# Sending the first layer's expert rows a chunk at a time instead of a batch at a time

## The chip, the cores and the metric

One NeuronCore of a Trainium2 chip runs the whole kernel. The metric is device time in microseconds (us), the median of several executions. Besides them one execution was taken by the hardware profiler.

## The reference, cut to what matters

Sixteen batches of 112 tokens, 256 wide, go through four residual blocks: cross attention with 16 heads over 375 keys, a top-2 mixture of 8 experts with a capacity of 560 rows an expert, a masked attention with one head, and a second top-2 mixture. The change lies at the seam of the first two:

```
x = x + xattn0(layernorm(x), ctx)            # 16 heads, 375 keys
# then, for t = layernorm(x) seen as T = 1792 tokens:
logits = t @ wr.T;  vals, idx = top_k(logits, 2);  gating = softmax(vals)
pos    = cumsum(mask) - 1;  keep = mask & (pos < 560)
xg     = rows of t gathered expert by expert (8 x 560)
x      = x + segment_sum(gate * (gelu(xg @ w1 + b1) @ w2 + b2))
```

## The kernel before, in words

The engines run separate programs that meet at semaphores. `attention0` is written as one long list of steps, `batch_order()`, which yields pairs (b, h) for b from 0 to 19 and h from 0 to 15. At step (b, h) TensorE (PE) makes the scores of head h of batch b, and, some steps behind, the probabilities (L505 to L508) and the values (L521) of an earlier head. The other engines walk the same list, each doing what its program names for a step. A pair (b, h) is thus a place in the order of an engine's queue and not a time: GpSimd (POOL), which has little to do, stands far ahead of PE and waits at its semaphores.

In the list of POOL stand, for each b: at h = 4 and 5 of odd b the norm of two coming batches (`pool_rsqrt`, `pool_normed`, L1715 to L1722), at h = 9 `context_lo(b + 2)` (L1749), which waits for ScalarE (ACT), at h = 10 the norm after attention of batch b - 2, which waits for VectorE (DVE), and `pool_scatter` for some (b, h).

Routing goes by chunks of batches, `CHUNKS0 = ((0, 4), (4, 4), (8, 4), (12, 2), (14, 1), (15, 1))`, as (first, count). When the logits of a chunk are there, DVE works out for its tokens the rows of the expert buffer that they go to (`dest`, L1167, semaphore `r_dest`) and the gates, which it writes beside the token in `XN` (L1194, semaphore `r_gate`). `pool_scatter(e, 0, b)` waits for both of the chunk of b and then issues two indirect DMAs (L1739), one for each of a token's two experts. Each writes 112 rows of 268 f32 words from `XN[:, b]` to `xg_scratch` in DRAM, 120 KB, so 240 KB a batch. Eight semaphores `d_sc` take turns: the DMAs of batch b wait until those of batch b - 4 have landed. All descriptors of POOL go through queue q0; the loads and stores that SP issues go through q1, on the same 16 DMA engines.

SP's part of attention 0 is a chain for each batch: `write_k` and `write_q` (L1941) store the split keys and queries to DRAM, `stack_k` (L1955) and `stack_q` (L1973) read them back in another layout into `KST` and `QST`, and `minima_rows` (L1982) writes two small rows into `QST` for each eight heads. PE waits for these at L483 and L505. After the last batch SP's `gathered(0)` (L2090) waits for all the scatters of the layer, and PE turns what it loads (L588).

`pvo_done` counts the turned values of a batch on DVE (L1363): its 17th is the one of batch 15.

Of the kernel before, what the change touches and what calls it, by code (L numbers as in the profile page):

```python
# [13 lines left out]
B, S, D, KEYS = 16, 112, 256, 375  # L14
# [45 lines left out]
CHUNKS0 = ((0, 4), (4, 4), (8, 4), (12, 2), (14, 1), (15, 1))  # L60
# [18 lines left out]
def build_kernel(nc, x, ctx_n, ctx_t, mask, bmask, wq, wk, wv, wo, wrt, w1, b1, w2, b2, gw, v1, v2, v3, const, out):  # L79
    top = ExitStack()  # L80
    with top:
# [3 lines left out]
        def sem(name):  # L85
            return top.enter_context(nc.semaphore(name))
# [91 lines left out]
        def expert_buffers(n):  # L178
# [41 lines left out]
        qk_done, min_done, pr_done, exp_done, pv_done, pvo_done, orm_done, xadd_done = (sem(n) for n in (  # L220
            "qk_done", "min_done", "pr_done", "exp_done", "pv_done", "pvo_done", "orm_done", "xadd_done"))
# [122 lines left out]
        def batch_order():  # L344

            return [divmod(n, H) for n in range(N + 4 * H)]
# [15 lines left out]
        def ends_chunk(b):  # L362
            return next((i for i, (b0, nb) in enumerate(CHUNKS0) if b0 + nb - 1 == b), None)
# [1347 lines left out]
        def pool_rsqrt(e, i, n, var_sem, rs_sem):  # L1711
            e.wait_ge(var_sem, n)
            if n > 2:
                e.wait_ge(rs_sem, n - 2)
            e.tensor_scalar(rs[:, i:i + 1], st2[:, i, 1:2], EPS, None, ALU.add).then_inc(eps, 1)  # L1715
            Chain.eps += 1
            e.wait_ge(eps, Chain.eps)
            e.tensor_tensor(rs[:, i:i + 1], rs[:, i:i + 1], epsm[:, 1:2], ALU.pow).then_inc(rs_sem, 1)

        def pool_normed(e, i, b, rs_sem, xn_sem):  # L1720
            e.wait_ge(rs_sem, b + 1)
            e.tensor_scalar(XN[:, b, 0:D], X[:, b, :], st2[:, i, 0:1], rs[:, i:i + 1], ALU.subtract, ALU.mult).then_inc(xn_sem, 1)  # L1722

        def pool_scatter(e, layer, b):

            dst, bound = ((xg_d, ROWS), (xg2_d, ROWS2))[layer]
            c = next(i for i, (b0, nb) in enumerate((CHUNKS0, CHUNKS1)[layer]) if b0 <= b < b0 + nb)
            e.wait_ge(r_dest, layer * len(CHUNKS0) + c + 1)
            e.wait_ge(r_gate, layer * len(CHUNKS0) + c + 1)
            if b == 0:  # L1730
                if layer == 0:
                    e.wait_ge(d_z, 16 * (E + 1))
                else:
                    e.wait_ge(d_z2, 16 * 2 * E)
            for d in range(2):
                n = 2 * (B * layer + b) + d
                if n >= 8:
                    e.wait_ge(d_sc[n % 8], 16 * (n // 8))
                e.indirect_dma_start(  # L1739
                    out=dst.ap()[0:bound, :], out_offset=bass.IndirectOffsetOnAxis(ap=dest[:, d, b:b + 1], axis=0),  # L1740
                    in_=XN[:, b, 0:RW], in_offset=None, bounds_check=bound - 1, oob_is_err=False).then_inc(d_sc[n % 8], 16)

        def pool_attention0(e):
            e.memset(CT[:, :, :, KEYS:KP], 0.0).then_inc(setup, 1)
            e.memset(epsm[:, 1:2], -0.5).then_inc(setup, 1)

            def context_lo(b):
                e.wait_ge(ch_done, b + 1)
                e.tensor_tensor(CL[:], CT[:, b % 2, :, :], CH[:], ALU.subtract).then_inc(cl_done, 1)  # L1749

            e.memset(VV[:, :, :, :, HD:HD + 1], 1.0).then_inc(setup, 1)
            e.memset(zero[:], 0.0).then_inc(setup, 1)
            e.wait_ge(setup, 4)
            e.memset(zero[:, :, RW_ID:RW_ID + 1], 1.0).then_inc(setup, 1)
            for i in range(2):
                e.wait_ge(setup, 5 + i)
                e.memset(KST[ROWS_KQ:ROWS_KQM, i].bitcast(F32), -1.0).then_inc(setup, 1)
            e.wait_ge(setup, 7)
            for b in range(2):
                pool_rsqrt(e, b, b + 1, var1, rs1)  # L1760
            e.memset(MK[:, 1, :].bitcast(F32), 0.0).then_inc(setup, 1)
            e.memset(XN[:, :, RW_ID:RW], 0.0).then_inc(setup, 1)
            e.iota(toki[:], [[S, B]], base=0, channel_multiplier=1).then_inc(setup, 1)
            e.wait_ge(setup, 10)
            e.tensor_copy(XN[:, :, RW_ID].bitcast(I32), toki[:]).then_inc(setup, 1)
            e.wait_ge(setup, 11)
            e.memset(QST[:, 1].bitcast(F32), 0.0).then_inc(stack_z, 1)
            e.wait_ge(stack_z, 2)
            e.memset(KST[ROWS_KQ:ROWS_KQM, 2].bitcast(F32), -1.0).then_inc(setup, 1)
            e.wait_ge(setup, 12)  # L1770
            for b in (2, 3):
                pool_rsqrt(e, b % 2, b + 1, var1, rs1)
            scattered_at = {(b + 7, 6): b for b in range(8)}
            scattered_at.update({(B - 1, 6): 8, (B - 1, 13): 9, (B, 6): 10, (B, 13): 11,
                                 (B + 1, 6): 12, (B + 1, 7): 13, (B + 2, 6): 14, (B + 3, 6): 15})
            for b, h in batch_order():
                if b + 2 < B and h == 9:
                    context_lo(b + 2)
                if b % 2 and b + 3 < B and h in (4, 5):
                    pool_rsqrt(e, h - 4, b + h, var1, rs1)  # L1780
                    pool_normed(e, h - 4, b + h - 1, rs1, xn1)
                if 2 <= b <= B + 1 and h == 10:
                    pool_rsqrt(e, 2 + (b - 2) % 2, b - 1, var2, rs2)
                    if b < B + 1:
                        pool_normed(e, 2 + (b - 2) % 2, b - 2, rs2, xn2)
                sent = scattered_at.get((b, h))
                if sent is not None:
                    if sent == B - 3:
                        e.wait_ge(pvo_done, B + 1)
                    pool_scatter(e, 0, sent)  # L1790

        def pool_experts(e, layer, between=None, beside=iter(())):
            base, per = (0, 4) if layer == 0 else (4 * E, 6)
# [399 lines left out]
        @block.gpsimd  # L2193
        def _(e):
            def first_block():
                pool_overflow_add(e, 0, range(5 * E - 5 - NY, 5 * E - 5))

            pool_attention0(e)
            pool_experts(e, 0, lambda: pool_roots(e, 1))
            pool_attention1(e, 2)  # L2200
            pool_experts(e, 1, first_block, pool_overflow_loads(e, 0))
            overflow_blocks(e, lambda j: pool_overflow(e, j))
# [53 lines left out]
```

## Time and profile before

| | |
|---|---|
| runs shown | 1006.34, 1006.79, 1010.84 us, median 1006.79 us |
| profiled execution | 1006.79 us, span 1004.7 us, so 2.1 us lie around the span |
| TensorE busy | 911.1 us, 91% of the span, 7913 matmuls |
| VectorE, ScalarE, GpSimd busy | 681.5, 439.0 and 473.9 us |
| mean granted TensorE clock | 0.959 |
| queue q0 / q1 of the DMAs | 18.33 / 140.40 MB, 9.1% / 52.6% of the 16 engines' span |

Attention 0 takes about the first 360 us, the first experts the next 230, attention 1 and its routing up to about 676, the second experts the rest.

How to read it: times are counted from the span's start. A busy share of PE is that of modelled, pipelined matmuls. A row of the timeline gives start, duration, engine, line, operation, output and input; in brackets stands how long the engine was idle ahead of it and what ended the idle time. A DMA that POOL issues shows up as the time that POOL takes over its descriptors, and not as that of the transfer.

### The profile page before, as it was taken

The page shows a single profiled execution, that of the slowest core. Times are in us where ns is not written, and L with a number is a line of the kernel's source. Part 1 is how long each engine was busy: PE and PEld are TensorE (multiplying, and loading weights), DVE is VectorE, ACT ScalarE, POOL GpSimd, SP SyncE. Part 2 cuts the span into 40 slices and gives each one's busy share as a digit, 9 for nine tenths or more (in the row PEclk, how much of TensorE's full clock was granted, in tenths as well). Part 3 has the DMA queues.
Part 4 walks back from the last instruction along what each step waited for, and adds up shares of the span by engine and source line. Part 5 has one row for each costly group of instructions (what it writes and reads, how often), then busy time and mean ns, then how long its engine had stood idle before and what let it go on. Part 6 is the DMA issues. An engine that isn't in the chain of part 4 may idle for free. (4 is left out here: it accounts for less than half of the span.)

```text
span 1004.7 us, 22213 instructions
## 1 busy us (share of the span) xinstructions
PE 911.1 (91%) x7913; PEld 839.8 (84%) x7913; DVE 681.5 (68%) x1988; ACT 439.0 (44%) x924; POOL 473.9 (47%) x443
## 2 busy tenths in 40 slices
PE   5799999999999749999999979838999999999996
PEld 5688988888888538999999957628999999999886
DVE  5667677667768448777777558846787777777353
ACT  3255555555554335555564434314333343442220
POOL 6024125244322426667666433672635655544513
PEclk8799999999999959999999999968999999999999
DMA  7998888797894167878977666634535465433202
GB/s 197 185 224 179 215 222 220 200 223 187 214 226 120 45 189 193 196 185 203 225 179 188 150 165 187 210 113 129 151 86 147 105 229 133 121 96 99 22 4 25
DMA packets 111840, 160.42 MB, mean 160 GB/s; under 512 B 12640, under 2 KB 100032, under 8 KB 109792
## 3 DMA queue, kind: packets, MB, share of 16 engines
q1 hardware_dynamic: 97776, 140.40, 52.6%
q0 software_dynamic: 13936, 18.33, 9.1%
q8 instruction: 78, 1.28, 0.5%
q14 instruction: 50, 0.41, 0.2%
HBM read 103.45 MB, written 56.96 MB: 160 GB/s over the span
## 5 line engine op out<-in xcount | busy, mean ns | idle before, releaser
L377 PE MATMUL ps<-XGH,WH 128*128 128x280 f32 (+1 forms) x768 | 220.2, 287 | 3.8 <-DVE GT L1488 2.4
L377 PE MATMUL ps<-XGL,WH 128*128 128x280 f32 (+1 forms) x768 | 221.1, 288 | 0.0
L377 PE MATMUL ps<-XGH,WL 128*128 128x280 f32 (+1 forms) x768 | 220.6, 287 | 0.0
L1804 POOL TENSOR_TENSOR HTL<-GT,HTH 128x280 fp32r<-128x280 f32 x112 | 114.5, 1024 | 164.8 <-DVE HTH L1492 164.8
L1341 DVE CUSTOM_DVE_ANT_0 NS<-ps,negm 112x375 f32<-112x375 f32 x256 | 135.2, 540 | 52.0 <-PE ps L483 48.6
L377 PE MATMUL ps<-WH,HTH 128*128 128x256 f32 (+1 forms) x536 | 152.8, 285 | 2.5 <-POOL HTL L1804 2.4
L377 PEld LDWEIGHTS ps<-XGH,WH 128*128 128x128 f32 x768 | 147.5, 192 | 5.2 <-DVE GT L1488 3.6
L377 PE MATMUL ps<-WL,HTH 128*128 128x256 f32 (+1 forms) x536 | 150.4, 281 | 0.0
L377 PE MATMUL ps<-WH,HTL 128*128 128x256 f32 (+1 forms) x536 | 150.2, 280 | 0.0
L377 PEld LDWEIGHTS ps<-XGH,WL 128*128 128x128 f32 x768 | 147.5, 192 | 0.0
L377 PEld LDWEIGHTS ps<-XGL,WH 128*128 128x128 f32 x768 | 147.1, 192 | 0.0
L876 ACT ACTIVATE PT<-ps 125x448 f32<-125x448 f32 x192 | 104.3, 544 | 76.8 <-PE ps L508 66.4
L1492 DVE CAST HTH<-GT 128x280 fp32r<-128x280 f32 x256 | 111.7, 443 | 16.4 <-ACT GT L949 9.6
L952 ACT ACTIVATE GT<-ps 128x280 f32<-128x280 f32 x128 | 51.7, 404 | 127.3 <-PE ps L377 124.8
L377 PEld LDWEIGHTS ps<-WH,HTH 128*128 128x128 f32 (+1 forms) x536 | 99.2, 185 | 3.5 <-DVE XG L1505 3.0
L483 PE MATMUL ps<-KST,QST 96*112 96x376 f32 x256 | 95.5, 379 | 4.5 <-DMA QST<-q_scratch 3.0
L377 PEld LDWEIGHTS ps<-WL,HTH 128*128 128x128 f32 (+1 forms) x536 | 99.5, 186 | 0.0
L377 PEld LDWEIGHTS ps<-WH,HTL 128*128 128x128 f32 (+1 forms) x536 | 99.3, 185 | 0.0
L1071 DVE TENSOR_TENSOR WL<-WG,WH 128x1024 fp32r<-128x1024 f32 x60 | 79.3, 1324 | 15.8 <-ACT WH L810 11.1
L1749 POOL TENSOR_TENSOR CL<-CT,CH 128x752 fp32r<-128x752 f32 x14 | 25.1, 1795 | 130.9 <-ACT CH L823 130.8
L1816 POOL DMA_INDIRECT out<-XG x40 | 67.1, 1678 | 38.1 <-DVE XG L1507 31.1
L810 ACT ACTIVATE WH<-WG 128x1024 fp32r<-128x1024 f32 x80 | 83.1, 1051 | 3.0 <-PE ps L377 3.0
(227 smaller groups left out, 1983.4 us busy)
## 6 DMA issues: line engine op xcount, KB each, us to landing
WG<-in_v SPq DMA_DIRECT2D x48, 512.0 KB
KST<-k_scratch SPq DMA_DIRECT2D x48, 376.0 KB
WG<-in_w SPq DMA_DIRECT2D x32, 512.0 KB
k_scratch<-KHL SPq DMA_DIRECT2D x64, 188.0 KB
CT<-in_ctx_t SPq DMA_DIRECT2D x28, 375.0 KB, 4.5
xg_scratch<-zero SPq DMA_DIRECT2D x8, 1289.8 KB
xg_scratch<-zero SPq DMA_DIRECT2D x16, 586.2 KB, 7.9
XG<-xg_scratch SPq DMA_DIRECT2D x14, 536.0 KB, 3.8
```

The lines of the kernel that those rows point to most:

```text
L377: m = e.matmul(out_ap, l, r, start=n == 0, stop=n == len(steps) - 1)
L483: e.matmul(ps[0:S, n % 3, 0:KP], QST[0:ROWS_KQ, b // 2 % 2, j // 4, up, j % 4, o:o + S], KST[0:ROWS_KQ, b % NKST, j, :], start=True, stop= ...
L810: e.activation(WH[n % NR][:], WG[:, n % NSTG, :], ACT.Copy).then_inc(wh_done, 1)
L876: e.activation(PT[:, k % 2, c, :], ps[0:KC, 3 + n % 2, 0:GQ], ACT.Exp, scale=-1.0).then_inc(exp_done, 1)
L952: e.activation(GT[:, gi % NG, :], ps[:, 2 * gi % 4, 0:HALF], ACT.Silu).then_inc(g_act[1], 1)
L1071: e.tensor_tensor(WL[n % NR][:], WG[:, n % NSTG, :], WH[n % NR][:], ALU.subtract).then_inc(wl_dve, 1)
L1341: e.tensor_tensor_reduce(out=NS[:, n % 2, :], in0=ps[0:S, n % 3, 0:KEYS], in1=negm[:], scale=1.0, scalar=3.0e38, op0=ALU.add, op1=ALU.min, ...
L1492: e.tensor_copy(HTH[:, f, cols], g).then_inc(hh[layer], 1)
L1749: e.tensor_tensor(CL[:], CT[:, b % 2, :, :], CH[:], ALU.subtract).then_inc(cl_done, 1)
L1804: e.tensor_tensor(HTL[:, f, cols], GT[:, gi % NG, :], HTH[:, f, cols], ALU.subtract).then_inc(hl_pool[layer], 1)
L1816: e.indirect_dma_start(out=(x_d.ap()[:, :], out2)[layer], out_offset=bass.IndirectOffsetOnAxis(ap=XG[0:rows_of(c), ex % 2, c, RW_ID:RW_ID ...
```

## The change

The table `scattered_at`, which gave each batch of the first layer a step for its scatter, goes. In its place a chunk's batches are sent in the list of four batches after its last one, at h = 6, 11, 13 and 15, or at h = 6 and 7 for b = 17. A wait for `pvo_done` ahead of the scatter of batch 13 goes too. The work is the same, 32 indirect DMAs in the same order.

| batch | step before | step after |
|---|---|---|
| 0, 1, 2, 3 | (7,6) (8,6) (9,6) (10,6) | (7,6) (7,11) (7,13) (7,15) |
| 4, 5, 6, 7 | (11,6) (12,6) (13,6) (14,6) | (11,6) (11,11) (11,13) (11,15) |
| 8, 9, 10, 11 | (15,6) (15,13) (16,6) (16,13) | (15,6) (15,11) (15,13) (15,15) |
| 12, 13, 14, 15 | (17,6) (17,7) (18,6) (19,6) | the same, without the wait at 13 |

```diff
@@ -1770,9 +1770,6 @@
             e.wait_ge(setup, 12)
             for b in (2, 3):
                 pool_rsqrt(e, b % 2, b + 1, var1, rs1)
-            scattered_at = {(b + 7, 6): b for b in range(8)}
-            scattered_at.update({(B - 1, 6): 8, (B - 1, 13): 9, (B, 6): 10, (B, 13): 11,
-                                 (B + 1, 6): 12, (B + 1, 7): 13, (B + 2, 6): 14, (B + 3, 6): 15})
             for b, h in batch_order():
                 if b + 2 < B and h == 9:
                     context_lo(b + 2)
@@ -1783,11 +1780,12 @@
                     pool_rsqrt(e, 2 + (b - 2) % 2, b - 1, var2, rs2)
                     if b < B + 1:
                         pool_normed(e, 2 + (b - 2) % 2, b - 2, rs2, xn2)
-                sent = scattered_at.get((b, h))
-                if sent is not None:
-                    if sent == B - 3:
-                        e.wait_ge(pvo_done, B + 1)
-                    pool_scatter(e, 0, sent)
+                turns = (6, 7) if b == B + 1 else (6, 11, 13, 15)
+                if b >= 4 and h in turns and ends_chunk(b - 4) is not None:
+                    b0, nb = CHUNKS0[ends_chunk(b - 4)]
+                    i = turns.index(h)
+                    if i < nb:
+                        pool_scatter(e, 0, b0 + i)
```

## Rows read from the trace of the kernel before

**Rows 1.** Engine times of the page: busy us, share of the span, instructions.

```profile
PE 911.1 (91%) x7913; PEld 839.8 (84%) x7913; DVE 681.5 (68%) x1988; ACT 439.0 (44%) x924; POOL 473.9 (47%) x443
```

**Rows 2.** Stretches: length, busy us (instructions) of each engine, clock, DMA share, GB/s.

```profile
176.00:180.00 4.00, 3.54 (x30) 3.26 (x23) 1.70 (x7) 1.57 (x4) 1.98 (x2) 1.00 0.94 237
...
256.00:260.00 4.00, 3.56 (x27) 3.38 (x26) 2.59 (x5) 2.94 (x6) 0.95 (x1) 1.00 1.01 266
...
280.00:284.00 4.00, 4.00 (x51) 3.63 (x51) 3.04 (x12) 1.82 (x5) 0.00 (x0) 1.00 1.08 236
...
332.00:336.00 4.00, 2.82 (x39) 2.34 (x40) 2.25 (x12) 2.63 (x7) 0.00 (x0) 1.00 0.08 24
```

**Rows 3.** Waits from 160 to 370 us: total us, times, longest.

```profile
ACT PT L876 <- remote: 3.6, 1, 3.6
...
PEld ps L505 <- DMA QST<-ML: 1.8, 4, 0.8
```

**Rows 4.** The same waits of PE's weight loads, from 280 to 300 us alone.

```profile
PEld ps L505 <- DMA QST<-ML: 0.8, 1, 0.8
PEld ps L483 <- DMA KST<-k_scratch: 0.6, 1, 0.6
```

**Rows 5.** Timeline of POOL, from batch 1's scatter to batch 6's.

```profile
176.06 1.03 POOL L1739 DMA_INDIRECT xg_scratch<-XN,dest  x1 [0.18 <-issue]
177.40 0.95 POOL L1739 DMA_INDIRECT xg_scratch<-XN,dest  x1 [0.30 <-issue]
192.43 1.81 POOL L1749 TENSOR_TENSOR CL<-CT,CH 128x752 fp32r<-128x752 f32 x1 [14.08 <-ACT CH L823]
...
254.89 1.03 POOL L1739 DMA_INDIRECT xg_scratch<-XN,dest  x1 [0.18 <-issue]
...
271.26 1.80 POOL L1749 TENSOR_TENSOR CL<-CT,CH 128x752 fp32r<-128x752 f32 x1 [14.09 <-ACT CH L823]
...
275.46 1.03 POOL L1739 DMA_INDIRECT xg_scratch<-XN,dest  x1 [0.18 <-issue]
```

**Rows 6.** Timeline of POOL, scatters of batches 8 to 15 and what stands between.

```profile
315.95 1.04 POOL L1739 DMA_INDIRECT xg_scratch<-XN,dest  x1 [4.13 <-issue]
...
326.59 1.03 POOL L1739 DMA_INDIRECT xg_scratch<-XN,dest  x1 [0.18 <-issue]
...
329.18 0.94 POOL L1739 DMA_INDIRECT xg_scratch<-XN,dest  x1 [0.30 <-issue]
330.42 0.94 POOL L1739 DMA_INDIRECT xg_scratch<-XN,dest  x1 [0.30 <-issue]
339.35 0.24 POOL L1715 TENSOR_SCALAR rs<-st 112x1 f32<-112x1 f32 x1 [7.99 <-DVE st L1290]
...
341.76 1.04 POOL L1739 DMA_INDIRECT xg_scratch<-XN,dest  x1 [0.18 <-DVE dest L1167]
...
349.34 0.94 POOL L1739 DMA_INDIRECT xg_scratch<-XN,dest  x1 [2.80 <-DVE OT L1363]
...
353.17 0.24 POOL L1715 TENSOR_SCALAR rs<-st 112x1 f32<-112x1 f32 x1 [1.65 <-DVE st L1290]
...
360.65 0.94 POOL L1739 DMA_INDIRECT xg_scratch<-XN,dest  x1 [3.98 <-DVE dest L1167]
361.89 0.94 POOL L1739 DMA_INDIRECT xg_scratch<-XN,dest  x1 [0.30 <-issue]
```

**Rows 7.** Timeline of DVE: gates of chunks 2 and 3, rows of chunk 5.

```profile
314.90 0.19 DVE L1194 TENSOR_TENSOR XN<-r_x 112x32 f32<-112x32 f32 x1
...
342.36 0.18 DVE L1194 TENSOR_TENSOR XN<-r_x 112x16 f32<-112x16 f32 x1
...
359.69 0.17 DVE L1167 TENSOR_SCALAR dest<-tq 112x2 int32<-112x2 f32 x1
```

**Rows 8.** Timeline of SP's queue: DMAs as issued.

```profile
290.24 1.25 SPq L1955 DMA_DIRECT2D KST<-k_scratch  x3
...
364.61 1.40 SPq L2090 DMA_DIRECT2D XG<-xg_scratch  x3
```

## The prediction

> **What bounds the kernel now.** I read the engine times first: TensorE is busy for 91% of the span [rows 1], so a gain has to take away one of its waits, and a loss has to make one. Then I read the stretches in which scatters are issued now or will be. In attention 0 PE is busy for 3.5 to 4.0 of each 4 us, at the full clock, while the 16 DMA engines are busy for 0.94 to 1.08 of the time [rows 2]. (A share over 1 is two queues' packets counted together.) From about 320 us on this turns over: the DMA engines are nearly idle (0.08), and PE's work is broken by waits. So there are two places to look at. One is the middle of attention 0, where moved transfers could make SP's loads late. The other is the end, where the last scatter releases the gather of the experts. Third come the waits of 160 to 370 us: DMAs that PE waits for are small there, 1.8 us over four waits for the minima rows [rows 3], the longest of them, 0.8 us, between 280 and 300 us, where the one wait for keys stands too, 0.6 us [rows 4]. Last, the timelines of POOL, DVE and SP's queue tell which scatter is late for what.
>
> **The end first, since it sets when the experts start.** The last two scatters start at 360.65 and 361.89 [rows 6]. The first was released by the `dest` of chunk 5, which DVE finishes at 359.86 [rows 7]. The gather goes out at 364.61 [rows 8], 1.78 us after POOL is done with the last one (361.89 + 0.94). All of this hangs on DVE's chain for batch 15, and none of it on POOL's place in its list. POOL is idle for 3.98 us ahead of it. The change leaves step (19,6) as it is. Cost: 0, as long as POOL reaches that step before 359.86, and now it reaches it 3.98 us early.
>
> **The scatters one by one.** A pair takes 1.34 us from its first start to its second [rows 5], and in a row without a wait the starts are 1.25 us apart [rows 6]. Four in a row have that pitch from 327.93 to the end of the 330.42 one, so I count 2.5 us for a pair that is added to a row.
>
> - Chunk 0. Batch 1 starts at 176.06 right behind the norm of step (7,10), though its step was (8,6): POOL is far ahead. In the new list it has the same place. Batches 2 and 3 follow at 178.65 and 181.15, until 183.3. The next work of POOL, L1749, waits for ACT until 192.43 after 14.08 us of idle time [rows 5]. Of that idle time 5.0 us are now filled, and 9 us are left. Cost to POOL's successors: 0. Without that cover it would be 5.0 us on the way to the next key projection.
> - Chunk 1 has the same form: batch 5 stays at 254.89, batches 6 and 7 come at 257.5 and 260.0, until 262.1. The next L1749 waits until 271.26, 14.09 us idle, 9 left. Cost 0.
> - Chunk 2. Batch 8 waits for its gates, done at 315.09 [rows 7], and starts at 315.95, 0.86 us later. Batch 9 sits behind the norm of (15,10), which waits for DVE. It stays at 326.59, with batch 10 at 329.18, and batch 11 moves from 341.76 to 331.67, until 333.9. POOL's next operation waits for DVE until 339.35 with 7.99 us of idle time [rows 6]. Cost 0: 5.5 us are left.
> - Chunk 3. Its gates are done at 342.54 [rows 7]. With the 0.86 us of chunk 2, batch 12 starts at 343.40 and batch 13, with no wait for DVE's turned values, at 345.95 instead of 349.34, and POOL is free at 348.1. The next, the root at 353.17, waits for DVE. Gain: 0 on any path, since batch 14 is behind that root and batch 15 behind its `dest`. The 2.80 us that the removed wait costs POOL are only turned into idle time a little later.
>
> Five pairs move far (2, 3, 6, 7, 11), two a little (12, 13), nine not at all. The semaphores `d_sc` add no wait: inside a group of four batches eight DMAs use eight different ones, and the batch four places back went out over 15 us earlier each time (the closest are 9 at 326.59 and 13 at 345.95).
>
> **What the transfers themselves cost.** A pair is 2 x 112 x 268 x 4 bytes, 0.24 MB. Two pairs more, 0.48 MB, fall into 178 to 184, where the engines move about 237 GB/s, and again into 257 to 262, at 266 GB/s [rows 2]. If the engines have no room at all, everything that SP has under way then lands up to 0.48 / 0.237 = 2.0 and 0.48 / 0.266 = 1.8 us later. That is 3.8 us as the upper bound, if PE was waiting for just that in both. Nothing in the waits says that it is: the minima rows hold PE up by at most 0.8 us at a time, and the keys once, between 280 and 300 us [rows 3, 4]. I take 0.2 us.
>
> On the other side four pairs leave places that are as full. Batch 6's went out at 275.46 [rows 5], ahead of the stretch from 280 with a DMA share of 1.08 [rows 2]. In that stretch the keys of batch 14 are written, and only at 290.24 does SP get to load them again [rows 8]. PE's one wait for keys, 0.6 us, and its longest for minima rows, 0.8 us, stand around it [rows 4]. The lower bound is both gone, -1.4 us. I take -0.4 us, nearer to zero, because 0.24 MB is one microsecond of a backlog of several.
>
> Sum: 1006.79 (the profiled execution, which is also the median of the runs) + 0 (end) + 0 (POOL) + 0.2 - 0.4 = 1006.6 us.
>
> The Trainium skill, DMA: Bandwidth & Descriptors, "Queues, rings and completion order", says that each DMA engine takes turns between the queues that have work, a packet at a time. By that rule a burst on q0 gets its turn ahead of whatever lies queued on q1, minima rows too. It speaks against this change, and no row of before separates the two queues at such a moment. By the rule the sum would have the 3.8 us of the next part.
>
> **The rivals.**
>
> 1. The bursts make PE wait. Mechanism: 0.48 MB of q0 is served between SP's packets at 178 to 184 and 257 to 262, the stores of keys and queries and the rows behind them land later, and PE stands at L483 or L505. For it: shares of 0.94 and 1.01 already. Against it: `stack_k` is issued about ten us ahead of its batch, and the waits seen come at other times. Price 2.0 + 1.8 = 3.8 us, 1010.6 us. It decides once the loads have less than 2 us in hand. It passes the half per cent (5.0 us) only if keys and queries both come late in one burst.
> 2. ACT's one wait that the profile calls remote, 3.6 us [rows 3], lies from 328.8 to 332.4. It contains the descriptors of batch 10 (329.18 to 331.36), and PE runs dry behind it. Should POOL's issuing be what holds ACT there, then the third pair in a row lengthens it by its 2.5 us, 1009.3 us. Against it: it is the only wait so named, and the other 30 indirect DMAs of this layer lie beside ACT's work without one. Should it be a matter of chance, it can as well be gone, -2.7 us or 1004.1 us.
> 3. The removed wait pays: batch 13's descriptors and DVE's chain for batch 15 (turned values at 347.8, then scale and turn back) no longer lie on each other at 349.3. Price: if a DVE step of 0.4 us was doubled by it, -0.4 us, 1006.4 us. Or the reverse, a clash with PE's last values before 347.8, +0.5 us.
> 4. The change does less than it says, because the list gives only an order: true for nine of 16 pairs, and already in the sum.
>
> **How the numbers follow.** The forecast, nothing that can be measured, has 0.70; rival 1 has 0.13, rival 2 longer 0.05 and shorter 0.04, rival 3 within the forecast's width 0.08. A measurement of this kernel can tell a change from none at about 0.5%, 5.0 us. No single mechanism reaches that. I leave 0.07 for slower by more (rival 1 with both loads late) and 0.03 for faster. The range: below, 1006.6 less the rest of the 1.4 us that can be gained and a microsecond for the runs' own spread, 1004.6; above, the full 3.8 us of rival 1, 1010.6, which also takes in the highest of the runs shown.
>
> **What would show it.** In the changed kernel's timeline of POOL scatters stand in rows at 176 to 183, 255 to 262 and 327 to 334, 1.25 us apart, with 9, 9 and 5.5 us of idle time behind them; no scatter near 208, 215, 275, 293. Batch 12 starts at about 343.4, batch 13 at about 346. The last two stand at 360.65 and 361.89, and the gather at 364.6, give or take a microsecond. The waits of L505 and L483 for DMAs stay under 3 us together. It is wrong if L1749 or the roots start behind a scatter instead of behind ACT or DVE, if PE's waits for `KST` or `QST` grow by microseconds right after 184 or 262, or if the gather of the experts starts over a microsecond later while DVE's chain does not.

## The result, and the profile after

| | before | after |
|---|---|---|
| median of 6 runs each, same chip | 1009.29 us (1006.34 to 1017.53) | 1020.58 us (1013.70 to 1025.14) |
| ratio, with 95% interval | | 1.011 (1.0077 to 1.0145) |
| profiled execution / its span | 1006.79 / 1004.7 us | 1021.98 / 1020.0 us |

The changed kernel is slower by 1.1%, about 11 us. The forecast was 1006.6 us and no change.

The engine times of the page do not show it. PE was as busy as before [rows 1], over a longer span:

```profile
PE 917.8 (90%) x7913; PEld 845.7 (83%) x7913; DVE 680.0 (67%) x1988; ACT 440.5 (43%) x924; POOL 474.9 (47%) x443
```

The timeline of POOL, to be held against [rows 5] and [rows 6], tells where the time is. The columns are start, duration, engine, line, operation.

```profile
175.26 1.03 POOL L1739 DMA_INDIRECT xg_scratch<-XN,dest  x1 [0.18 <-issue]
...
181.60 0.94 POOL L1739 DMA_INDIRECT xg_scratch<-XN,dest  x1 [0.30 <-issue]
...
196.71 1.82 POOL L1749 TENSOR_TENSOR CL<-CT,CH 128x752 fp32r<-128x752 f32 x1 [14.16 <-ACT CH L823]
...
264.94 0.94 POOL L1739 DMA_INDIRECT xg_scratch<-XN,dest  x1 [0.30 <-issue]
...
276.27 1.81 POOL L1749 TENSOR_TENSOR CL<-CT,CH 128x752 fp32r<-128x752 f32 x1 [10.39 <-ACT CH L823]
...
330.44 1.03 POOL L1739 DMA_INDIRECT xg_scratch<-XN,dest  x1 [0.17 <-issue]
...
336.79 0.95 POOL L1739 DMA_INDIRECT xg_scratch<-XN,dest  x1 [0.30 <-issue]
...
349.58 0.24 POOL L1715 TENSOR_SCALAR rs<-st 112x1 f32<-112x1 f32 x1 [11.85 <-DVE st L1290]
...
353.65 1.03 POOL L1739 DMA_INDIRECT xg_scratch<-XN,dest  x1 [1.84 <-issue]
...
357.49 0.94 POOL L1739 DMA_INDIRECT xg_scratch<-XN,dest  x1 [0.30 <-issue]
...
372.36 0.94 POOL L1739 DMA_INDIRECT xg_scratch<-XN,dest  x1 [3.97 <-DVE dest L1167]
```

POOL does what was foretold: unbroken rows with starts 1.25 us apart (2.15 us once, at 261.54), and idle time behind each. But what it waits for comes later. L1749 of step (8,9) started at 192.43 and is now at 196.71, that of (12,9) was at 271.26 and is at 276.27, the root of (16,10) was at 339.35 and is at 349.58. POOL is not late: it is idle for 14, 10 and 12 us ahead of these. ACT and DVE are late.

Behind the row at 176 the kernel is 5.0 us later than ahead of it (the step ahead, L1749 of (7,9), came 0.7 us early), behind the row at 257 it is 2.3 us, behind the one at 330 6.4 us, and by the gather another 1.5. Between the rows 2.7 us come back. The gather of the experts starts at 376.36 instead of 364.61 [rows 8], 11.75 us late.

The waits of 160 to 370 us, to be held against [rows 3] (total, times, longest), name the loss:

```profile
ACT PT L876 <- remote: 8.5, 3, 6.5
...
DVE NS L1341 <- issue: 5.8, 4, 4.5
...
DVE OT L1363 <- remote: 4.2, 1, 4.2
...
ACT KHL L839 <- remote: 1.7, 2, 0.9
...
PEld ps L505 <- DMA QST<-ML: 1.3, 2, 1.0
```

The wait for the minima rows is smaller than before, 1.3 us for 1.8, and none for keys is left. So SP's transfers are not what came late. What has grown are waits put down to "remote" or "issue", which is no engine of this core and no DMA that the profile shows (before had 3.6 us of them for ACT's PT and 3.0 us for DVE's NS). The long ones stand beside the rows. ACT is held from 332.6 to 339.15, while POOL issues from 330.44 to 337.74. DVE is held from 355.35 to 359.55, with POOL issuing from 353.65 to 358.43. In each the engine goes on 1.1 to 1.4 us after the last issue has ended. The 3.6 us of [rows 3] fit in: they end at 332.40, 1.0 us after the row of four that ends at 331.36.

TensorE shows best what is missing. A group at L521 is 24 matmuls of one head group, with no wait inside. Timeline of PE in the changed kernel:

```profile
181.27 0.56 PE L521 MATMUL ps<-PT,VV 125*17 125x112 f32 x10
182.63 0.39 PE L521 MATMUL ps<-PT,VV 125*17 125x112 f32 x4 [0.81 <-issue]
184.07 0.54 PE L521 MATMUL ps<-PT,VV 125*17 125x112 f32 x10 [1.05 <-issue]
```

The same group in the kernel before, where no scatter is under issue:

```profile
182.64 0.77 PE L521 MATMUL ps<-PT,VV 125*17 125x112 f32 x24
```

24 matmuls took 0.77 us there and 3.34 us here, in pieces of 10, 4 and 10 with pauses between. No semaphore stands between them. So it isn't data that is late, it is the next instruction. That the supply of instructions fails is my reading of this. The page lists the transfers of instructions as DMA queues of their own, alike in both kernels (packets, MB, share):

```profile
q8 instruction: 78, 1.28, 0.5%
q14 instruction: 50, 0.41, 0.2%
```

None of these packets lies between 179.5 and 184, between 334 and 340, or between 354 and 360 us of the changed trace, and yet a held engine goes on within each of these stretches. So no such packet is seen to end these stalls, and what does stays open.

Then TensorE's clock takes its share. Stretches of PE in the changed kernel (length, busy us of PE, PEld, DVE, ACT, POOL, clock, DMA share, GB/s):

```profile
180.00:184.00 4.00, 2.21 (x26) 1.69 (x25) 0.63 (x3) 1.03 (x2) 1.94 (x3) 1.00 1.03 314
184.00:188.00 4.00, 3.93 (x26) 3.65 (x26) 2.76 (x9) 1.84 (x5) 0.00 (x0) 0.58 0.58 137
188.00:192.00 4.00, 4.00 (x38) 3.27 (x37) 1.83 (x5) 1.09 (x2) 0.00 (x0) 0.57 0.71 183
...
264.00:268.00 4.00, 3.33 (x40) 2.28 (x39) 2.35 (x7) 1.82 (x4) 1.57 (x2) 1.00 0.70 226
...
336.00:340.00 4.00, 0.26 (x1) 0.26 (x2) 0.14 (x1) 0.85 (x4) 1.43 (x2) 0.78 0.24 75
340.00:344.00 4.00, 4.00 (x37) 3.34 (x37) 2.29 (x14) 1.40 (x3) 0.00 (x0) 0.50 0.01 2
344.00:348.00 4.00, 4.00 (x34) 3.05 (x33) 0.55 (x3) 1.09 (x2) 0.00 (x0) 0.50 0.00 0
```

After two of the stalls the granted clock goes from 1.00 to 0.50, that is from 2.4 to 1.2 GHz, and stays there for most of 184 to 192 and all of 340 to 348, though PE has work again. Behind the row at 257, where PE's values come in pieces too, it stays at 1.00. What half the clock costs is seen on a whole group of 24, which takes 1.32 us instead of 0.77:

```profile
340.86 1.32 PE L521 MATMUL ps<-PT,VV 125*17 125x112 f32 x24
```

So a stall is paid about twice where the clock falls: the group at 181.27 took 2.6 us longer and L1749 came 5.0 us later; ACT's wait at 333 grew by 2.9 us and the root behind it came 6.4 us later. Without a fall of the clock the row at 257 cost 2.3 us.

Of the 15.3 us between the two spans 11.75 are there when the gather starts. The other 3.6 come up later, in parts that are the same in both kernels. They lie inside the spread of one kernel's runs (11 us for before), and I can't put them down to the change: from the gather to the end of the span before took 640.1 us and the changed kernel 643.6, while in f2 and f1 below, again before and changed, it was 646.2 and 641.5.

### The profile page after: what moved, and what is told of

It reads as the page before. It is cut to its first block and busy times, and to the rows that moved or that the text cites. A ratio compares the mean times of both kernels' runs of the same rounds, so it can differ in the third digit from the quotient of the medians.

```text
span 1020.0 us, 22212 instructions
## 1 busy us (share of the span) xinstructions
PE 917.8 (90%) x7913; PEld 845.7 (83%) x7913; DVE 680.0 (67%) x1988; ACT 440.5 (43%) x924; POOL 474.9 (47%) x443
## 5 line engine op out<-in xcount | busy, mean ns | idle before, releaser
L1492 DVE CAST HTH<-GT 128x280 fp32r<-128x280 f32 x256 | 107.9, 429 | 16.8 <-ACT GT L949 8.2
L1749 POOL TENSOR_TENSOR CL<-CT,CH 128x752 fp32r<-128x752 f32 x14 | 25.2, 1797 | 131.9 <-ACT CH L823 131.8
L1495 DVE TENSOR_TENSOR HTL<-GT,HTH 128x280 fp32r<-128x280 f32 x144 | 82.7, 574 | 5.0
```

Of the source, the lines that this page charges most:

```text
L1492: e.tensor_copy(HTH[:, f, cols], g).then_inc(hh[layer], 1)
L1495: e.tensor_tensor(HTL[:, f, cols], g, HTH[:, f, cols], ALU.subtract).then_inc(hl_dve[layer], 1)
```

## The experiments

The experiments ran in six groups (e, f, g, h, i, j), each on another chip, and all are timed against the kernel before, run beside them on that chip. A "quiet" chip below is one on which before took about 1000 us, a "loud" one is one on which it took about 1010. I did not choose which I got, and it turned out to be the main thing. The numbers behind a ratio are its 95% interval. Of the edits only the lines that matter are shown.

**One part of the change at a time, and a paced version.** The edits of the first three, and of the fourth in `pool_scatter`:

```diff
 e1  -                    if sent == B - 3:
     -                        e.wait_ge(pvo_done, B + 1)
 e2  -            scattered_at = {(b + 7, 6): b for b in range(8)}
     +            scattered_at = {(4 * (b // 4) + 7, (6, 11, 13, 15)[b % 4]): b for b in range(8)}
 e3  -  (B - 1, 6): 8, (B - 1, 13): 9, (B, 6): 10, (B, 13): 11,
     +  (B - 1, 6): 8, (B - 1, 11): 9, (B - 1, 13): 10, (B - 1, 15): 11,
 e4  on the changed kernel
     +            if layer == 0 and b:
     +                for n in (2 * b - 2, 2 * b - 1):
     +                    e.wait_ge(d_sc[n % 8], 16 * (n // 8 + 1))
```

> The kernel before with one thing of the change: the wait for the turned values ahead of batch 13's scatter is gone; the table is the old one. Theory S (an engine runs out of instructions while a row of four or more indirect DMAs is under way, and TensorE's clock then falls): batches 11, 12 and 13 now make a row of six from 341.8 to about 349, where before it was four and a gap of 2.8 us, so the stall around 343 to 348 grows by 1 to 3 us: ratio 1.001 to 1.003. Theory V (what costs is the bytes that the moved pairs put beside SP's transfers between 176 and 262 us): nothing, ratio 1.000.

> The kernel before with the new places for batches 0 to 7 alone. Both theories: a loss. In the changed kernel context_lo of step (12,9) came at 276.3 instead of 271.3, 5.0 us late. Theory S: 4 to 7 us, ratio 1.004 to 1.007, with PE's trickle in the values (L521) near 182 and 265 and no wait for KST or QST behind it. Theory V: the same, but as waits of L483 and L505 for KST and QST.

> The kernel before with the new places for batches 8 to 11 alone; a row of six indirect DMAs from about 326.6 to 334, at a time when the DMA engines are nearly idle. Theory S: ACT's remote wait grows from 3.6 to about 6.5 us and TensorE works at half clock behind it, 5 to 7 us in all, ratio 1.005 to 1.007; some of it comes back since batches 12 and 13 are then no row of six with 11. Theory V: nothing, ratio 1.000, since there is nothing that the bytes could hold up.

> The changed kernel, with each scatter of the first layer made to wait until both DMAs of the batch ahead of it have landed, so that never more than one pair is under way. The same bytes at nearly the same places, each pair some 2 to 3 us later than in a row. Theory S: the stalls go, no remote wait over 1 us, and the time is that of before or less, ratio 0.996 to 1.001. Theory V: still slower than before, 1.008 to 1.012, since the bytes fall into the same stretches.

A quiet chip: before 1000.71 us. e1 0.9995 (0.9967 to 1.0024), e2 0.9992 (0.9966 to 1.0017), e3 0.9983 (0.9962 to 1.0004). None of the three costs anything that can be measured, and no trace of e1 to e3 has a remote wait from 160 to 370 us. My theory (S) had foretold a loss in e2 and e3 and missed both; theory V missed e2. e4 was slower, 1.0044 (1.0016 to 1.0071), which neither theory had. Its gather starts at 360.70, where traces of before and of the changed kernel on such a chip (f2 and f1, below) have 355.02 and 356.38. Its trace tells where some of that is lost. The pauses make batch 11's scatter so late that POOL's norm follows right behind it, at 337.76, and TensorE waits for POOL (timeline of PE in e4):

```profile
340.16 0.39 PE L391 MATMUL ps<-cst,XN 112*128 112x112 f32 x2 [2.27 <-POOL XN L1722]
```

Behind the pauses of batches 12 to 15 POOL still waits for DVE, for 1.93 and 4.09 us, so these are not seen to cost anything.

**The whole change again.** f1 is the changed kernel, f2 the kernel before, both unaltered; f3 is the changed one with the removed wait put back:

```diff
                     if i < nb:
+                        if b0 + i == B - 3:
+                            e.wait_ge(pvo_done, B + 1)
                         pool_scatter(e, 0, b0 + i)
```

> The changed kernel, nothing altered, run beside the kernel before once more. In the call of its parts alone neither part cost anything and no engine showed a remote wait. Theory S1 (a row of scatters starves an engine of instructions only on some chips or in some executions): on a chip like that of the last call the ratio is 0.998 to 1.003 and the trace has no remote wait over 1 us; on a chip like the first it is 1.008 to 1.014. Theory S2 (it takes all parts of the change together, by where each instruction then stands in an engine's stream): 1.008 to 1.014 on any chip, with the remote waits near 183, 263, 333 and 356 us.

> The kernel before, nothing altered, for a trace on the chip of this call and as a measure of what two equal kernels differ by here. All theories: ratio 0.997 to 1.003. If the chip matters, its trace differs from the first one of before by the 3.6 us of ACT's remote wait at 328.8, and the span by some us.

> The changed kernel with the wait for the turned values put back ahead of batch 13's scatter. Theory S2: the row of four with batches 12 and 13 is broken, so DVE's remote wait of 4.2 us at 355 goes; 1 to 3 us less than the changed kernel. Theory S1: like the changed kernel within 0.3%.

Quiet once more: before 999.18 us. f1 1.0007 (0.9983 to 1.0031), f2 1.0007 (0.9980 to 1.0033), f3 0.9993 (0.9969 to 1.0018). The change costs nothing here. The timeline of PE in f1, where the row of six runs from 178.6 to 185.9, has the group inside the row whole, and the one behind it too:

```profile
183.72 0.77 PE L521 MATMUL ps<-PT,VV 125*17 125x112 f32 x24
187.11 0.77 PE L521 MATMUL ps<-PT,VV 125*17 125x112 f32 x24
```

And the stretch of f1 in which its row runs keeps PE full at the full clock, with as much on the DMA engines as in the changed kernel's first trace (0.99 against 1.03):

```profile
180.00:184.00 4.00, 4.00 (x41) 3.76 (x43) 1.96 (x7) 2.45 (x6) 3.09 (x4) 1.00 0.99 274
```

So neither the order of instructions nor the bytes make the stall by themselves; it takes a loud chip. ("Loud" names what is seen, not a cause.)

**A third time, and twice the scatters.** g2 is the changed kernel unaltered. g1 issues each scatter of batches 4 to 11 twice, the second time into a spare tensor. That tensor, and a later wait that counts the added DMAs, are not shown:

```diff
+            if layer == 0 and 4 <= b < 12:
+                for d in range(2):
+                    e.indirect_dma_start(
+                        out=spare_d.ap()[0:bound, :], out_offset=bass.IndirectOffsetOnAxis(ap=dest[:, d, b:b + 1], axis=0),
+                        in_=XN[:, b, 0:RW], in_offset=None, bounds_check=bound - 1, oob_is_err=False).then_inc(d_ow[0], 16)
```

> The changed kernel, nothing altered, a third time. Two calls had the kernel before at 999 to 1001 us and no remote waits in any kernel; the first had it at 1009 and the changed one at 1021. Theory S1 (it depends on the chip or its state whether a row of scatters stops other engines): if the kernel before stands near 1009 again, the changed one stands at 1.008 to 1.014 with remote waits; if it stands near 1000, the ratio is 0.998 to 1.003 without them. Theory N (the first ratio was a chance of that call): 0.998 to 1.003 wherever before stands.

> The changed kernel with every scatter of batches 4 to 11 issued twice, the second time into a spare tensor: rows of 12 and 14 indirect DMAs, 15 to 18 us long, in place of 6 and 8. The output is the same. Theory S1 on a chip that shows no stalls: POOL is late for context_lo of (12,9) by nothing (9 us of idle time against 10 us of added issue, so 1 us at most), for the root of (16,10) by some 2 us, ratio 1.000 to 1.004. On a chip that shows them: remote waits of 10 us and more, 1.025 or above. Theory L (the length of a row decides, and the quiet chip only starts later): stalls on the quiet chip too, 1.008 or above.

A loud chip: before 1011.94 us. g2 1.0092 (1.0055 to 1.0129): the first result again, so that was no chance. g1 1.0325 (1.0267 to 1.0383). Eight more pairs cost 23 us over g2, 2.9 us each, where a pair takes 2.5 us to issue. Timeline of ACT in g1, its three longest stalls:

```profile
257.34 0.55 ACT L877 ACTIVATE PT<-ps 125x448 f32<-125x448 f32 x1 [4.54 <-remote]
...
268.11 0.48 ACT L840 ACTIVATE KHL<-ps 128x376 fp32r<-128x376 f32 x1 [6.52 <-remote]
...
368.07 0.54 ACT L877 ACTIVATE PT<-ps 125x448 f32<-125x448 f32 x1 [10.26 <-remote]
```

The row at 350.6 has twelve DMAs and ends at 365.4; ACT's stall of 10.26 us ends 2.7 us after it. At this place, that of batches 9 to 11, rows of 4, 6 and 12 held ACT for 3.6, 6.5 and 10.3 us: the longer the row, the longer the stall. Elsewhere the length is not all. The stall of 4.54 us stands beside a row of four, that of 6.52 us ends inside a row of twelve (260.87 to 276.60), and in the changed kernel the rows of six at 176 and 257 held ACT for no more than 1.0 us at a time.

**Rows broken up, and plain DMAs.** h1 and h2 have the lines of e4 with a condition that spares the tail, from batch 12 on in h1, on the changed kernel, and from batch 14 on in h2, on the kernel before. h3 and h4 add four plain DMAs of the same 112 rows of 268 words to the kernel before (the spare tensor and the waits that count these DMAs are not shown):

```diff
 h1  +            if layer == 0 and 1 <= b < 12:     (then as e4, on the changed kernel)
 h2  +            if layer == 0 and 1 <= b < 14:     (then as e4, on the kernel before)
 h3  in pool_attention0, behind the scatter of batch 8
     +                        for i in range(4):
     +                            e.dma_start(spare_d.ap()[i], XN[:, i, 0:RW]).then_inc(d_ow[0], 16)
 h4  in sp_attention0, at the end of b = 14
     +                    e.wait_ge(r_gate, 3)
     +                    for i in range(4):
     +                        e.dma_start(spare_d.ap()[i], XN[:, i, 0:RW]).then_inc(d_o, 16)
```

> The changed kernel; each scatter of batches 1 to 11 waits until both DMAs of the batch ahead have landed, so that up to batch 11 at most one pair is under way. The tail (12 to 15) is as changed. Theory R (what stops the other engines is a row of indirect DMAs, more the longer it is unbroken): where the kernel before stands near 1010, the stalls at 183, 262 and 333 us go or shrink to those of single pairs, and the ratio is 0.995 to 1.002 instead of 1.010; where before stands near 1000, 0.999 to 1.003. Theory V (the bytes alone): 1.008 to 1.014 near 1010.

> The kernel before; each scatter of batches 1 to 13 waits until the one ahead has landed. Only the rows 9-10 and 11-12 of before are broken up by it. Theory R: where before stands near 1010, ACT's remote wait of 3.6 us and PE's trickle at 343 to 348 shrink, ratio 0.993 to 0.998: faster than both kernels. Where it stands near 1000, 0.999 to 1.002. Theory V: 0.999 to 1.002 everywhere.

> The kernel before with four more DMAs from POOL right behind batch 8's scatter: plain ones, 112 rows of 268 words each as a scatter has, from XN into a spare tensor, so a row of six from 316 to 323 us. The output is the same. Theory G (it is POOL's making of descriptors and its queue that stops the others, indirect or not): near 1010, remote waits around 318 to 325 us and 3 to 6 us more, 1.003 to 1.006; near 1000 nothing over 1.001. Theory I (only indirect DMAs do it): 1.000 near 1010 too.

> The same four plain DMAs, the same rows and bytes at about the same time (315 to 318 us), but issued by SP on its own queue. The output is the same. Theory G: no remote wait at 318 to 325, ratio 0.999 to 1.002 whatever before stands at (0.7 us at most for the minima rows queued behind them). Theory V (traffic of many small packets, whoever issues it): like h3, 1.003 to 1.006 near 1010.

A loud chip again: before 1011.43 us. h1 0.9963 (0.9932 to 0.9995), h2 0.9953 (0.9929 to 0.9977). The changed kernel with its rows broken up loses nothing, where without pauses it lost 0.9 and 1.1% on the two other loud chips (it did not run unaltered on this one). It has the same bytes in nearly the same places. h2 breaks up only the two rows of four that before has itself, and gains 4.7 us on it (the median is 5.2 lower). The timeline of POOL in h2 shows the pauses, 3.22 us and 2.48 us in place of 0.30:

```profile
324.87 0.95 POOL L1742 DMA_INDIRECT xg_scratch<-XN,dest  x1 [0.30 <-issue]
329.04 0.94 POOL L1742 DMA_INDIRECT xg_scratch<-XN,dest  x1 [3.22 <-issue]
...
340.75 0.94 POOL L1742 DMA_INDIRECT xg_scratch<-XN,dest  x1 [2.48 <-issue]
```

Its trace has no remote wait from 160 to 370 us, and ACT's 3.6 us of [rows 3] are gone; h1 has one, DVE's of 1.7 us. The gain of h2 is found in DVE's timeline too. From the rows of chunk 2 to those of chunk 4 (L1167, 313.04 to 350.60 in the first trace of before) it took 37.6 us in before, 32.8 in h2 and 31.6 in f2 on the quiet chip. So the kernel before loses some 6 us of its own to its two rows of four on a loud chip.

The pauses do two things at once, and the runs do not part them: they break the row of issues, and they keep the pairs under way to one. They also do not end all stalls. Beside single pairs too ACT is held on loud chips, in h2 at 272.91 and 290.55 for 1.6 us each, and once for longer (timelines of ACT in h2 and h3; POOL issues batch 6 in h2 from 272.52 to 274.81, batch 7 in h3 from 293.68 to 295.96):

```profile
272.91 0.49 ACT L839 ACTIVATE KHL<-ps 128x376 fp32r<-128x376 f32 x1 [1.55 <-issue]
...
297.18 0.48 ACT L840 ACTIVATE KHL<-ps 128x376 fp32r<-128x376 f32 x1 [3.48 <-remote]
```

In none of the twelve traces from quiet chips has ACT or DVE such a wait of over 1 us between 160 and 350 us.

And pauses can make POOL late with its own work. In h1 PE waits 2.4 us for the norm behind batch 11, as in e4. In h2 the norm behind batch 13 starts right behind the scatter, at 347.79, and PE waits 6.7 us for what follows from it, where it is 2.7 us in h1.

h3 0.9978 (0.9950 to 1.0006), h4 1.0011 (0.9986 to 1.0037): plain DMAs cost nothing from either queue. POOL gets a plain one out in 0.54 us and an indirect one in 1.25 us (POOL's timeline of h3):

```profile
320.49 2.18 POOL L1795 DMA_DIRECT2D spare_scratch<-XN  x4
```

ACT works on beside these four. In the same trace it stalls for 3.7 us at batch 10's scatter and, as shown, for 3.5 us at batch 7's: the chip was loud. This speaks for the indirect form and against POOL's queue as such, with one limit. Four plain ones make a row of 2.2 us, shorter than four indirect ones.

**Descriptors or bytes.** i1 is g1 with `in_=XN[:, b, 0:8]` and a spare tensor of 8 words a row. i2 and i3 are e2 and e3 again, j1 and j2 are g1 and i1 again.

> The changed kernel with every scatter of batches 4 to 11 issued twice, as in the doubled kernel, but the second one of each moves 8 words a token instead of 268: the same number of indirect DMAs and of packets, 3% of the bytes. The output is the same. Where the kernel before stands near 1010: theory M (making and fetching the descriptors of indirect DMAs is what stops the others): like the doubled kernel, 1.025 to 1.035. Theory W (their bytes, written in scattered rows): like the changed one, 1.008 to 1.014. Near 1000: 0.999 to 1.004.

> The kernel before with the new places of batches 0 to 7 alone, once more. Where before stands near 1010: the rows of six at 176 and 255 us cost 4 to 7 us, ratio 1.004 to 1.007; context_lo of (12,9) about 5 us late. Near 1000: 0.997 to 1.003, as the first time.

> The kernel before with the new places of batches 8 to 11 alone, once more. Where before stands near 1010: the row of six at 326 makes ACT's remote wait 6.5 us instead of 3.6 and lets TensorE's clock fall to half, which costs 4 to 7 us, 1.004 to 1.007. Near 1000: 0.997 to 1.003.

> The kernel with every scatter of batches 4 to 11 issued twice, once more. Where the kernel before stands near 1010: 1.025 to 1.040 as the first time. Where it stands near 1000: the thin form of it cost 0.8% there; theory S1 (no engine is starved on such a chip; POOL is late with its own work) gives 1.005 to 1.012 with no remote wait over 1 us; theory L (the length of a row decides on any chip) gives 1.02 or more, with remote waits.

> The kernel with the thin second scatters (8 words a token), once more. Where before stands near 1010: theory M (descriptors) 1.025 to 1.040, like the doubled kernel; theory W (bytes) 1.010 to 1.020, the changed kernel's loss and POOL's own lateness. Near 1000: 1.005 to 1.011, as the first time, and the difference from the doubled kernel in the same call is what the bytes cost there.

Both chips were quiet (998.24 and 998.97 us), so the question put to a loud chip got no answer. i2 0.9994 (0.9968 to 1.0019) and i3 0.9996 (0.9965 to 1.0027) repeat e2 and e3. i1 1.0080 (1.0052 to 1.0107), twice what I had expected at most for a quiet chip, j1 1.0067 (1.0042 to 1.0092), j2 1.0078 (1.0039 to 1.0117). On a quiet chip even rows of 12 starve no engine: j1 has no remote wait. Its loss is POOL's own lateness, which shows up with a name. Timeline of PE in j1:

```profile
341.33 0.61 PE L392 MATMUL ps<-cst,XN 112*128 112x112 f32 x2 [5.06 <-POOL XN L1723]
```

Full and thin rows cost the same there, within their intervals.

## Why the prediction was wrong

**What POOL does, and what its idle time covers:** right. The rows, their pitch and the idle time behind them came as foretold, no work of POOL started behind a scatter that had started behind ACT or DVE before, and no `d_sc` wait was added. The starts themselves were later by what the others had lost.

**The end at no cost:** right in its links, wrong in its time. Batch 15's scatter still waits 3.97 us for `dest`, and the gather still follows it. All of it came 11.7 us later.

**The transfers, rival 1:** the mechanism did not show. Waits for minima rows fell from 1.8 to 1.3 us, and e2, with both bursts, cost nothing on two quiet chips. The rule of the Trainium skill (DMA: Bandwidth & Descriptors, "Queues, rings and completion order") may hold on the DMA engines: from 179.5 to 184 us of the changed trace the packets of q0 and q1 took 51.1% and 52.8% of their time, which fits turns but does not show them. Here it held up nothing that PE waited for. One reading of this part was wrong without changing the sum: a share over 1 is not always that of two queues, for from 280 to 284 us of before q1 alone stands at 101.4%.

**Rival 2, the failed step.** The prediction saw the wait named remote, saw that it contained batch 10's descriptors, and priced the possibility that the third pair would lengthen it by 2.5 us. It lengthened by 2.9 us, to 6.5. So the mechanism was on the list, with 0.05, and the step that failed is the evidence against it, "the other 30 indirect DMAs of this layer lie beside ACT's work without one". Most of those stood in pairs, and the other row of four went unread: at 341.8 to 346.5 before has one too, and the last 12 of 48 matmuls of PE's values come in four pieces from 345.2 to 347.8, with a pause of about 0.4 us ahead of each. Two rows of four, and both had a stall. It does not even hold for all pairs: beside batch 7's (293.05 to 295.33) ACT was held for 1.55 us in a wait named issue and not remote. Timelines of ACT and PE in the kernel before:

```profile
294.17 0.48 ACT L839 ACTIVATE KHL<-ps 128x376 fp32r<-128x376 f32 x1 [1.55 <-issue]
...
343.32 1.53 PE L521 MATMUL ps<-PT,VV 125*17 125x112 f32 x36
345.23 0.35 PE L521 MATMUL ps<-PT,VV 125*17 125x112 f32 x3 [0.38 <-issue]
...
347.41 0.39 PE L521 MATMUL ps<-PT,VV 125*17 125x112 f32 x4 [0.44 <-issue]
```

And I priced it in one place instead of four, and without the clock, which in two of them then stays at half for 7 and 9 us of work. The measured terms are 5.0, 2.3, 6.4 and 1.5 us less the 2.7 us won back between and the 0.7 us that the kernel was early: 11.8 us in place of 2.5.

**The chips.** Of the six chips with experiments two were loud, and so was the one of the result. The prediction has no term for the chip. The statement that nothing measurable happens is true on the quiet ones (f1: 1.0007) and false on the loud ones (1.011 and 1.0092). The kernel before shows in its own trace which it is, by the remote wait and by its time.

**What stays open:** what makes a chip loud (the chip, the core on it, or what else goes on there); whether the making of descriptors or the bytes of the indirect DMAs does it, which the thin rows would have told on a loud chip; whether it is the unbroken issuing or the number of pairs under way; why single pairs hold ACT in some places and not in others; whether the thing missing is really the supply of instructions; and how the loss divides on a loud chip when each row is moved alone.

## What to carry to other kernels

Do not issue indirect DMAs in unbroken rows beside engines that are busy, even if the issuing engine and the DMA engines have time to spare: let each pair wait for the one before it, as h2 does (0.9953 of before on a loud chip), but count the time that the pauses add to the issuing engine, and keep them away from work of its own that others wait for (e4, 1.0044 on a quiet chip). A wait that the profile can't name, next to a row of descriptors, deserves a price of its own, counted once for every row that the change makes, and with the clock that TensorE loses by it. And a ratio measured on one chip may be another on the next: keep the time of the unchanged kernel beside it.

## What the runs showed of the hardware that was not expected

- On some chips or occasions, rows of four to twelve indirect DMAs stop ScalarE and VectorE for up to 10 us and make TensorE issue in pieces (24 matmuls in 3.34 us instead of 0.77); the longest stall beside each of the rows of 4, 6 and 12 at one place ended 1.0, 1.4 and 2.7 us after the last issue. Single pairs held ScalarE for 1.6 us in some places, once for 3.5 us. On other chips rows of twelve do nothing of the kind (j1).
- The same kernel took 998 to 1001 us on four occasions and 1009 to 1012 us on three.
- After two stalls of PE the granted clock was 0.50 for 6.8 us (184.6 to 191.4) and 8.7 us (339.7 to 348.4) in which PE had work all the time; after a third, near 266, it stayed at 1.00.
